# Two of four block merges moved into later links of the recurrence, and the mask add of the next sequence moved to a step's end

## The chip, the cores and the metric

The kernel runs on one core of a Trainium2 chip. The metric is the device time of one execution in microseconds. Each core has TensorE (PE: matrix products; PEld is its loading of weights), VectorE (DVE), ScalarE (ACT) and GpSimdE (POOL); each works through its own queue of instructions in order, and they wait for each other on semaphores. SyncE (SP) issues the DMAs here.

## The reference

One layer in float32, for 8 sequences of 512 tokens and width 128: a layer norm, an attention part with 8 heads of 64, a residual, and a mixture of experts. The attention is a gated delta rule in 8 modes per head. Keys and queries are turned by a mode's own angles; then, per head and mode:

```python
def step(S, inp):
    q_t, k_t, v_t, b_g, b_beta = inp
    S = S * jnp.exp(b_g)[..., None, None]
    kv = jnp.einsum('mbhk,mbhkv->mbhv', k_t, S)
    dv = (v_t[None] - kv) * b_beta[..., None]
    S = S + k_t[..., :, None] * dv[..., None, :]
    o_t = jnp.einsum('mbhk,mbhkv->mbhv', q_t, S)
    return (S, o_t)
```

The modes' outputs are summed with softmax weights.

## The kernel before

There are three stages. `prepare` (until some 810 us of the profiled execution) makes norms, projections, decay sums and angle tables. `recurrence` (until some 4640 us) runs the delta rule. `experts` does the rest. The change touches `recurrence` alone.

`recurrence` goes over 64 (head, batch) sequences of 512 tokens. The 8 modes lie as 4 pairs (`PAIRS`) on 128 partitions. A sequence is cut into 8 spans (`SUPER`) of 64 tokens. Within a span the rule is solved at once: a 64 x 64 lower-triangular system, whose inverse is built from 32 x 32 blocks. Between spans a chain of 8 links carries the state `S`.

`emit` writes a loop body of 8 steps. In step k the chain of one sequence runs while the next sequence is prepared. The bodies are: one step that only prepares (first sequence), then 7 passes of a loop (one per head) with 8 steps each, then a last body of 8. Each ends with an all-engine barrier (`fresh`).

Preparing, in order: VectorE turns keys and queries (`rotate`, L773 to L781, from `kqT`), four quarters. TensorE computes eight blocks of scores (`scores`, L929 and L933) into `SP`; ScalarE makes the decay factors of each block in place in `DB` (`exponential(c)`, L681, four instructions); VectorE multiplies both into `SC` (`take_scores`, L806), and needs for block c the scores and the exponential of c. `DB` is loaded with decay sums; GpSimdE adds `below`, the mask above the diagonal, to all of it first (L864). After the eighth block VectorE inverts the 32 x 32 diagonal blocks (`to_lanes`, then `eliminate`, L822 and L823, 30 rounds of two), and writes them back by two transposes: `TM` (L834) and `XO` (L835, `from_lanes`). The last L823 raises `lanes_done`.

Running begins with that inverse. The 64 x 64 inverse needs its lower left block, `-inverse x scores x inverse`, in two rounds m, for two halves g of the spans (g = 0 is spans 0 to 3, g = 1 is 4 to 7). `merge(0, g)` on TensorE (L910, 64 recorded products of 32 x 32) reads `TM` and the old scores in `SC` and writes `PR[g]`; ScalarE's `merged(0, g)` takes it, negated, into `ZM` (L659); `merge(1, g)` (L912, 64 recorded products) takes `ZM` and `XO`; `merged(1, g)` copies it into `XN` (L661). `first_block(e)` copies `XO` into `XN` (L665). Semaphore `act_m` counts these six on ScalarE.

A link c of the chain is, on TensorE: `solve_values` (L970), `read_state` (L958), `outputs` (L1001, L1011), `solve_reads` (L979), `keep_state` (L984), `write_state` (L994); on ScalarE: R (L726), Sdec (L730), the W copy (L733, waits for `solve_reads`), the S copy (L739, waits for `write_state`). Links 0 to 3 need half g = 0 alone, links 4 to 7 half g = 1.

The order of each queue is written out by hand. `jobs` is a list of the work that isn't chain; `PE_PLACES` and `ACT_PLACES` hold, for each link, how many jobs go to its two places. On TensorE the places of link c are ahead of `solve_reads(c)` (for c = 0 ahead of `solve_values(0)`) and behind `keep_state(c)`, ahead of `write_state(c)`. On ScalarE they are behind the W copy and behind the S copy.

Before, TensorE does merges (0,0), (0,1), (1,0) ahead of the links; then score block 0, `solve_values(0)`, merge (1,1), score block 1, `write_state(0)`; block 2, `solve_reads(1)`, `keep_state(1)`, block 3, `write_state(1)`; blocks 4 and 5, then 6 in link 2; block 7 in link 3 ahead of `solve_reads(3)`. ScalarE does `first_block(0)`, (0,0), `first_block(1)`, (0,1), exponential 0, (1,0), exponentials 1 and 2; (1,1) behind W copy 0, exponential 3 behind S copy 0, 4 and 5 in link 1, 6 and 7 in link 2 (7 behind its S copy).

Of the kernel before, what the change touches and what calls it, by code (L numbers as in the profile page):

```python
# [489 lines left out]
def recurrence(nc, sems, fresh, c_mat, ident, KQ_s, V_s, G_s, EG_s, COL_s, TAB_s, O_s):  # L490

    GROUP = SUPER // 2
    with ExitStack() as ctx:
# [61 lines left out]
        def emit(n0, h0, odd, steps, first=False):  # L555
# [17 lines left out]
            with nc.Block() as block:  # L573
# [74 lines left out]
                def _(act):  # L648
                    token_rows = PR[0][:, :].rearrange("p (z a f) -> p z a f", z=2, a=PAIRS)
                    for k, (runs, prepares, more) in enumerate(steps):  # L650
                        now, par = parts(k)

                        def merged(m, g):

                            cs = slice(GROUP * g, GROUP * g + GROUP)
                            act.wait_ge(pe_m, 4 * k + 2 * m + g + 1)
                            got = PR[g][:, :].rearrange("p (a c i) -> p a c i", a=PAIRS, c=GROUP)
                            if m == 0:
                                act.activation(ZM[:, :, cs, 0:C], got, ACT.Copy, scale=-1.0).then_inc(act_m, 1)  # L659
                            else:  # L660
                                act.copy(XN[:, :, cs, C:], got).then_inc(act_m, 1)  # L661
# [14 lines left out]
                        def exponential(c):  # L676
                            if c == 0:
                                act.wait_ge(d_ready, k + 1)
                                act.wait_ge(l_col, 16 * (k + 1))
                            for p in range(PAIRS):  # L680
                                last = act.activation(DB[:, p, c, :], DB[:, p, c, :], ACT.Exp, bias=col[:, par, 0, p, c:c + 1])  # L681
                            last.then_inc(d_exp, 1)
# [12 lines left out]
                        if runs:  # L695
# [5 lines left out]
                            merged(0, 1)  # L701
                            if prepares:
                                exponential(0)
                            merged(1, 0)
                            if prepares:
                                exponential(1)
                                exponential(2)
                        jobs = [lambda: merged(1, 1)] if runs else []
                        if prepares:
                            ex = [lambda c=c: exponential(c) for c in range(3 if runs else 0, SUPER)]  # L710
                            keys = [lambda c=c: token_keys(c) for c in range(SUPER)]
                            turn = [(lambda r=r: transposed(k + sets, r)) if more else (lambda: None) for r in range(4)]
                            jobs += ex + keys[0:4] + turn[0:2] + keys[4:6] + turn[2:3] + keys[6:8] + turn[3:4]
                        if not runs:
                            for job in jobs:
                                job()
                        else:
                            plan = ACT_PLACES if prepares else [1] + [0] * (2 * SUPER - 1)
# [136 lines left out]
                def _(pool):  # L855
                    for k, (_, prepares, _) in enumerate(steps):
                        if not prepares:
                            continue
                        if k:

                            pool.wait_ge(lanes_done, k)
                        here(pool, l_gr, 4, k)
                        every = DB[:, :, :, :].rearrange("p a c i -> p (a c) i")
                        pool.tensor_tensor(every, every, bcast(below[:, :], 1, PAIRS * SUPER), ALU.add).then_inc(d_ready, 1)  # L864

                @block.tensor
                def _(pe):
                    wins = turned = 0
                    token_rows = PR[0][:, :].rearrange("p (z a f) -> p z a f", z=2, a=PAIRS)
                    for k, (runs, prepares, more) in enumerate(steps):  # L870
# [20 lines left out]
                        def merge(m, g):  # L891

                            if m == 0 and k:
# [3 lines left out]
                                else:  # L897
                                    pe.wait_ge(act_t, 4 * turned)
                            if m == 1:
                                pe.wait_ge(act_m, 6 * k + 2 + 2 * g)  # L900
# [36 lines left out]
                        def token_keys(c2):  # L937
# [4 lines left out]
                            elif runs:  # L942
                                pe.wait_ge(act_m, 6 * k + 5)
# [17 lines left out]
                        def solve_values(c):  # L961
# [3 lines left out]
                            if c % GROUP == 0:  # L965
                                pe.wait_ge(act_m, 6 * k + 5 + c // GROUP)
# [47 lines left out]
                        if first and k == 0:  # L1014
                            wins += 1
                            for r in range(4):
                                transposes(0, r)
                        if runs:
                            merge(0, 0)
                            merge(0, 1)  # L1020
                            merge(1, 0)
                        jobs = [lambda: merge(1, 1)] if runs else []
                        if prepares:
# [5 lines left out]
                            jobs = sc[0:1] + jobs + sc[1:] + kd[0:2] + turn[0:2] + kd[2:3] + turn[2:3] + kd[3:4] + turn[3:4]  # L1029
# [3 lines left out]
                        else:  # L1033
                            plan = PE_PLACES if prepares else [0, 1] + [0] * (2 * SUPER - 2)
# [26 lines left out]
        PE_PLACES = [1, 2, 1, 1, 2, 1, 1, 1, 0, 0, 1, 1, 1, 1, 1, 1]  # L1061
        ACT_PLACES = [1, 1, 1, 1, 1, 1, 0, 0, 1, 1, 1, 2, 1, 1, 2, 0]
# [305 lines left out]
```

## Time and profile before

| | |
|---|---|
| median of 3 runs | 5335.73 us (5333.28 to 5338.02) |
| the profiled execution | 5332.65 us |
| its span, first to last instruction | 5331.1 us |
| mean granted TensorE clock | 0.835 |
| busy PE, PEld, DVE, ACT, POOL | 4090.7, 3347.1, 3758.0, 2856.6, 413.9 us |

Times in rows are us from the span's start. An entry such as `x64` counts instructions; `[1.70 <-DVE run_TM L834]` is idle time of the engine ahead of the instruction and what ended it. The granted clock is 1.00 for 2.4 GHz and 0.50 for 1.2 GHz. Ends of matrix products are modelled, so I go by starts where I can.

### The profile page before, as it was taken

The numbers are of one execution on the slowest core, as the hardware profiler recorded it, in microseconds if no ns is written. First come the engines' busy times: TensorE is split into PE (matmuls) and PEld (weight loads), VectorE is DVE, ScalarE is ACT, GpSimd is POOL, SyncE is SP. The second block draws the span as 40 slices with busy tenths as digits, with TensorE's granted clock in tenths as the row PEclk, the third lists the DMA queues.
The fourth block names the chain that finished last, engine by engine and source line by source line (L and its number), as shares of the span: only waits on it lengthen the run. The fifth ranks groups of instructions, "written<-read, shape, count | busy, mean of one in ns | idle before, by whom it ended". The sixth has DMA issues, their size and how long they took to land. (4 is left out here: it accounts for less than half of the span.)

```text
span 5331.1 us, 196493 instructions
## 1 busy us (share of the span) xinstructions
PE 4090.7 (77%) x85809; PEld 3347.1 (63%) x85809; DVE 3758.0 (70%) x7820; ACT 2856.6 (54%) x9665; POOL 413.9 (8%) x164
## 2 busy tenths in 40 slices
PE   3333006989899889989989998989899889868778
PEld 1111005777777777777777777777777777744445
DVE  3333558888888788878878887887888888534444
ACT  3333224666666666666666665666666666522222
POOL 0000321000100010000000010000100010000000
PEclk7666557888888898888889888988888889878888
DMA  2333342222222322322222222222222222120110
GB/s 62 85 85 83 143 172 60 50 63 80 50 50 60 81 51 50 88 54 50 48 81 58 52 82 47 50 63 79 50 50 63 78 50 50 24 54 14 28 28 16
DMA packets 275624, 331.13 MB, mean 62 GB/s; under 512 B 132440, under 2 KB 179424, under 8 KB 266592
## 3 DMA queue, kind: packets, MB, share of 16 engines
q1 hardware_dynamic: 274784, 318.75, 23.0%
q8 instruction: 671, 10.99, 0.9%
q14 instruction: 169, 1.38, 0.1%
HBM read 232.70 MB, written 85.98 MB: 60 GB/s over the span
## 5 line engine op out<-in xcount | busy, mean ns | idle before, releaser
L823 DVE TENSOR_TENSOR run_XL<-run_XL,run_EL 128x30 f32<-128x30 f32 (+14 forms) x1920 | 637.3, 332 | 65.9
L822 DVE TENSOR_TENSOR run_EL<-run_AL,run_XL 128x30 f32<-128x30 f32 (+14 forms) x1920 | 636.1, 331 | 66.0
L806 DVE TENSOR_TENSOR run_SC<-run_SP,run_DB 128x512 f32<-128x512 f32 x512 | 349.9, 686 | 455.7 <-PE run_SP L933 449.5
L929 PE MATMUL run_SP<-run_KP 64*32 64x128 f32 x8192 | 624.9, 302 | 23.9 <-DVE run_SC L806 10.4
L864 POOL TENSOR_TENSOR run_DB<-run_DB,run_below 128x2048 f32<-128x2048 f32 x64 | 297.2, 4644 | 3495.1 <-DVE run_XL L823 2993.9
L681 ACT ACTIVATE run_DB<-run_DB,run_col 128x64 f32<-128x64 f32 x2048 | 537.2, 337 | 13.6 <-POOL run_DB L864 5.9
L887 PE MATMUL run_PR<-ident,run_win 128*64 128x128 f32 x4096 | 303.7, 285 | 305.0 <-DMA run_win<-KQ_s 280.9
L929 PEld LDWEIGHTS run_SP<-run_KP 64*32 64x32 f32 x8192 | 467.5, 119 | 100.6 <-issue 53.1
L688 ACT ACTIVATE run_KD<-run_PR,run_col 128x64 f32<-128x64 f32 x2048 | 469.7, 326 | 12.9 <-PE run_PR L949 6.8
L739 ACT COPY run_S<-run_KS 128x256 f32<-128x256 f32 x448 | 166.7, 372 | 564.9 <-PE run_KS L994 564.9
L933 PE MATMUL run_SP<-run_KP 64*32 64x64 f32 x8192 | 454.5, 243 | 0.0
L887 PEld LDWEIGHTS run_PR<-ident,run_win 128*64 128x64 f32 x4096 | 242.1, 142 | 335.8 <-DMA run_win<-KQ_s 281.3
L726 ACT ACTIVATE run_R<-run_KS,run_col 128x64 f32<-128x64 f32 x1792 | 414.6, 322 | 70.6 <-PE run_KS L958 70.4
L773 DVE TENSOR_TENSOR run_tmpv<-run_tab,run_kqT 128x512 f32<-128x512 f32 x512 | 383.1, 748 | 76.0 <-issue 27.5
L912 PE MATMUL run_PR<-run_XO,run_ZM 32*64 32x32 f32 x8192 | 404.7, 268 | 26.6 <-ACT run_ZM L659 24.7
L730 ACT ACTIVATE run_Sdec<-run_S,run_decay 128x64 f32<-128x64 f32 x1536 | 413.4, 364 | 0.0
L912 PEld LDWEIGHTS run_PR<-run_XO,run_ZM 32*64 32x64 f32 x8192 | 387.8, 194 | 40.1 <-ACT run_ZM L659 29.6
L970 PE MATMUL run_WP<-run_V,run_XN 64*64 64x64 f32 x8192 | 374.3, 238 | 9.8 <-issue 9.0
L949 PE MATMUL run_PR<-ident,run_KP 64*64 64x64 f32 x8192 | 297.0, 222 | 95.9 <-ACT run_KD L688 90.5
L1001 PE MATMUL run_OB<-run_W,run_SC 128*64 128x64 f32 x4096 | 360.9, 234 | 0.5 <-ACT run_W L733 0.5
L949 PEld LDWEIGHTS run_PR<-ident,run_KP 64*64 64x64 f32 x8192 | 262.7, 135 | 150.4 <-issue 146.2
L979 PE MATMUL run_WP<-run_R,run_XN 64*64 64x64 f32 x7168 | 307.6, 224 | 53.6 <-ACT run_R L726 34.0
(201 smaller groups left out, 7817.7 us busy)
## 6 DMA issues: line engine op xcount, KB each, us to landing
run_DB<-G_s SPq DMA_DIRECT2D x256, 256.0 KB, 4.7
run_EG<-EG_s SPq DMA_DIRECT2D x128, 512.0 KB, 8.5
TAB_s<-tab_tab SPq DMA_DIRECT2D x16, 2048.0 KB, 6.3
run_tab<-TAB_s SPq DMA_DIRECT2D x32, 1024.0 KB, 10.8
KQ_s<-proj_win SPq DMA_DIRECT2D x32, 768.0 KB
run_win<-KQ_s SPq DMA_DIRECT2D x64, 384.0 KB
run_V<-V_s SPq DMA_DIRECT2D x128, 128.0 KB, 2.6
V_s<-proj_vv SPq DMA_DIRECT2D x64, 128.0 KB
```

Source lines behind the costliest of these rows:

```text
L681: last = act.activation(DB[:, p, c, :], DB[:, p, c, :], ACT.Exp, bias=col[:, par, 0, p, c:c + 1])
L688: last = act.activation(KD[:, par, p, c, :], token_rows[:, c % 2, p, :], ACT.Copy, scale=col[:, par, 2, p, c:c + 1])
L726: last = act.activation(R[:, p, :], KS[:, 0, p, :], ACT.Copy, scale=col[:, now, 1, p, c:c + 1])
L730: last = act.activation(Sdec[:, p, :], S[:, c % 2, p, :], ACT.Copy, scale=decay[:, now, p, c:c + 1])
L773: v(dve.tensor_tensor(tmpv[:, query], tab[:, at, :, t], bcast(kqT[:, at, t], 1, PAIRS), ALU.mult))
L822: v.link(dve.tensor_tensor(e, bcast(AL[:, r + 1:, r], 2, done), bcast(XL[:, r, 0:done], 1, rows), ALU.mult))
L823: less = dve.tensor_tensor(XL[:, r + 1:, 0:done], XL[:, r + 1:, 0:done], e, ALU.subtract)
L887: last = pe.matmul(PR[1][64 * e:64 * e + 64, 128 * i:128 * i + 128], win[:, i, off:off + DK], ident[:, :], start=True, stop=True)
L912: last = pe.matmul(to[64 * e:64 * e + SPAN], ZM[two, p, c, :], XO[two, p, c, :], start=True, stop=True)
L929: pe.matmul(out[64 * e:64 * e + C, p].rearrange("p (z u) i -> p z (u i)", z=2), KP[f, par, p, t0:t1], KP[f, kq, p, t0:t0 + SPAN], start=Tr ...
L933: last = pe.matmul(out[64 * e + C:64 * e + SPAN, p, 0::3, :], KP[f, par, p, t1:t1 + C], KP[f, kq, p, t1:t1 + C], start=True, stop=True)
L949: last = pe.matmul(token_rows[f, z, p, :], KP[f, par, p, t0:t0 + SPAN], ident[f, f], start=True, stop=True)
```

## The change

On TensorE merges (0,0) and (1,0) stay ahead of the links; (0,1) goes between `solve_values(0)` and score block 1, and (1,1) between `keep_state(1)` and score block 3. `PE_PLACES[3]` becomes 2. On ScalarE `merged(0, 1)` goes behind W copy 0, `merged(1, 1)` behind W copy 1; exponentials 0 to 2 stay ahead of the links, 3 stays behind S copy 0, 4 is behind S copy 1, 5 and 6 in link 2, and 7 behind W copy 3 (`ACT_PLACES[6]` becomes 1). The waits on `pe_m` and `act_m` are counted anew. On GpSimdE the mask add for the next sequence is issued at the end of the step before, so that the one for a pass's first step is done ahead of the barrier.

```diff
                         def merged(m, g):
...
-                            act.wait_ge(pe_m, 4 * k + 2 * m + g + 1)
+                            act.wait_ge(pe_m, 4 * k + 2 * g + m + 1)
...
                             if c == 0:
-                                act.wait_ge(d_ready, k + 1)
+                                if k + sets:
+                                    act.wait_ge(d_ready, k + sets)
                                 act.wait_ge(l_col, 16 * (k + 1))
...
                             first_block(0)
                             merged(0, 0)
                             first_block(1)
-                            merged(0, 1)
+                            merged(1, 0)
                             if prepares:
                                 exponential(0)
-                            merged(1, 0)
-                            if prepares:
                                 exponential(1)
                                 exponential(2)
-                        jobs = [lambda: merged(1, 1)] if runs else []
+                        jobs = [lambda: merged(0, 1)] if runs else []
...
+                            if runs:
+                                jobs += ex[0:1] + [lambda: merged(1, 1)]
+                                ex = ex[1:]
                             jobs += ex + keys[0:4] + turn[0:2] + keys[4:6] + turn[2:3] + keys[6:8] + turn[3:4]
+                        elif runs:
+                            jobs += [lambda: None, lambda: merged(1, 1)]
...
-                            plan = ACT_PLACES if prepares else [1] + [0] * (2 * SUPER - 1)
+                            plan = ACT_PLACES if prepares else [1, 1, 1] + [0] * (2 * SUPER - 3)
...
                 @block.gpsimd
                 def _(pool):
-                    for k, (_, prepares, _) in enumerate(steps):
-                        if not prepares:
-                            continue
-                        if k:
-
-                            pool.wait_ge(lanes_done, k)
-                        here(pool, l_gr, 4, k)
+                    def only_below(loads):
+
+                        pool.wait_ge(l_gr, 16 * 4 * loads)
                         every = DB[:, :, :, :].rearrange("p a c i -> p (a c) i")
                         pool.tensor_tensor(every, every, bcast(below[:, :], 1, PAIRS * SUPER), ALU.add).then_inc(d_ready, 1)
+
+                    if first:
+                        only_below(1)
+                    for k, (_, prepares, more) in enumerate(steps):
+                        if more:
+
+                            pool.wait_ge(lanes_done, k + 1)
+                            only_below(k + 1 + sets)
...
-                                    pe.wait_ge(act_t, 4 * turned)
+                                    pe.wait_ge(act_t, 4 * turned_so_far)
                             if m == 1:
-                                pe.wait_ge(act_m, 6 * k + 2 + 2 * g)
+                                pe.wait_ge(act_m, 6 * k + 2 + 3 * g)
...
-                                pe.wait_ge(act_m, 6 * k + 5)
+                                pe.wait_ge(act_m, 6 * k + 4)
...
-                                pe.wait_ge(act_m, 6 * k + 5 + c // GROUP)
+                                pe.wait_ge(act_m, 6 * k + 4 + 2 * (c // GROUP))
...
+                        turned_so_far = turned
                         if runs:
                             merge(0, 0)
-                            merge(0, 1)
                             merge(1, 0)
-                        jobs = [lambda: merge(1, 1)] if runs else []
+                        jobs = []
...
-                            jobs = sc[0:1] + jobs + sc[1:] + kd[0:2] + turn[0:2] + kd[2:3] + turn[2:3] + kd[3:4] + turn[3:4]
+                            if runs:
+                                jobs = sc[0:1] + [lambda: merge(0, 1)] + sc[1:3] + [lambda: merge(1, 1)] + sc[3:]
+                            else:
+                                jobs = sc
+                            jobs += kd[0:2] + turn[0:2] + kd[2:3] + turn[2:3] + kd[3:4] + turn[3:4]
+                        elif runs:
+                            jobs = [lambda: merge(0, 1), lambda: merge(1, 1)]
...
-                            plan = PE_PLACES if prepares else [0, 1] + [0] * (2 * SUPER - 2)
+                            plan = PE_PLACES if prepares else [0, 1, 0, 1] + [0] * (2 * SUPER - 4)
...
-        PE_PLACES = [1, 2, 1, 1, 2, 1, 1, 1, 0, 0, 1, 1, 1, 1, 1, 1]
-        ACT_PLACES = [1, 1, 1, 1, 1, 1, 0, 0, 1, 1, 1, 2, 1, 1, 2, 0]
+        PE_PLACES = [1, 2, 1, 2, 2, 1, 1, 1, 0, 0, 1, 1, 1, 1, 1, 1]
+        ACT_PLACES = [1, 1, 1, 1, 1, 1, 1, 0, 1, 1, 1, 2, 1, 1, 2, 0]
```

## Rows read from the trace of the kernel before

**Rows 1.** The page: busy time per engine; costliest group that waits on scores.

```profile
PE 4090.7 (77%) x85809; PEld 3347.1 (63%) x85809; DVE 3758.0 (70%) x7820; ACT 2856.6 (54%) x9665; POOL 413.9 (8%) x164
...
L806 DVE TENSOR_TENSOR run_SC<-run_SP,run_DB 128x512 f32<-128x512 f32 x512 | 349.9, 686 | 455.7 <-PE run_SP L933 449.5
```

**Rows 2.** Line L834: its instructions (ns min/median/max, first and last start), who waited (us, times).

```profile
L834 DVE STREAM_TRANSPOSE run_TM<-run_XL x64: 2012/2080/2164, 854.7 to 4615.3; 128x1024 f32<-128x1024 f32 x64
...
  PEld run_PR L910: 70.4, 39
```

**Rows 3.** Timeline (start, length in us, engine, line, ...), VectorE, two steps.

```profile
1991.97 2.06 DVE L834 STREAM_TRANSPOSE run_TM<-run_XL 128x1024 f32<-128x1024 f32 x1
...
2048.31 2.04 DVE L834 STREAM_TRANSPOSE run_TM<-run_XL 128x1024 f32<-128x1024 f32 x1
2050.27 1.93 DVE L835 STREAM_TRANSPOSE run_XO<-run_XL 128x1024 f32<-128x1024 f32 x1
...
2082.68 0.69 DVE L806 TENSOR_TENSOR run_SC<-run_SP,run_DB 128x512 f32<-128x512 f32 x1 [2.69 <-PE run_SP L933]
...
2108.26 2.10 DVE L834 STREAM_TRANSPOSE run_TM<-run_XL 128x1024 f32<-128x1024 f32 x1
```

**Rows 4.** Timeline, TensorE, the second of these steps.

```profile
2050.41 2.36 PE L910 MATMUL run_PR<-run_TM,run_SC 32*32 32x32 f32 x128 [1.70 <-DVE run_TM L834]
2053.82 3.62 PE L912 MATMUL run_PR<-run_XO,run_ZM 32*64 32x32 f32 x64 [1.04 <-ACT run_ZM L659]
...
2081.54 0.30 PE L929 MATMUL run_SP<-run_KP 64*32 64x128 f32 x2
...
2082.53 0.68 PE L979 MATMUL run_WP<-run_R,run_XN 64*64 64x64 f32 x16
```

**Rows 5.** Timeline, ScalarE, around the eighth take of that step.

```profile
2080.29 1.06 ACT L681 ACTIVATE run_DB<-run_DB,run_col 128x64 f32<-128x64 f32 x4
...
2083.26 0.37 ACT L733 COPY run_W<-run_WP 128x256 f32<-128x256 f32 x1 [0.15 <-PE run_WP L979]
2085.45 0.37 ACT L739 COPY run_S<-run_KS 128x256 f32<-128x256 f32 x1 [1.82 <-PE run_KS L994]
```

**Rows 6.** Stretches: length; busy PE, PEld, DVE, ACT, POOL; granted clock; DMA share, GB/s.

```profile
2060.00:2064.00 4.00, 4.00 (x78) 3.82 (x78) 4.00 (x8) 0.44 (x2) 0.00 (x0) 0.50 0.01 4
```

**Rows 7.** Timeline, TensorE, merges at either clock, in three other steps.

```profile
1217.14 2.05 PE L912 MATMUL run_PR<-run_XO,run_ZM 32*64 32x32 f32 x64
...
2003.80 2.35 PE L912 MATMUL run_PR<-run_XO,run_ZM 32*64 32x32 f32 x64
...
4617.38 3.62 PE L910 MATMUL run_PR<-run_TM,run_SC 32*32 32x32 f32 x128 [4.38 <-DVE run_TM L834]
```

**Rows 8.** Stretches T + 12.6 to T + 17.0, the first and last of 62.

```profile
927.80:932.20 4.40, 4.40 (x82) 3.83 (x81) 3.67 (x7) 0.58 (x1) 0.00 (x0) 0.50 0.00 0
...
4569.90:4574.30 4.40, 4.40 (x120) 4.03 (x120) 4.40 (x9) 1.74 (x6) 0.00 (x0) 0.84 0.00 0
```

**Rows 9.** Timeline, VectorE and TensorE, two steps in which the chain came late.

```profile
1688.58 2.07 DVE L834 STREAM_TRANSPOSE run_TM<-run_XL 128x1024 f32<-128x1024 f32 x1
1696.01 1.18 PE L912 MATMUL run_PR<-run_XO,run_ZM 32*64 32x32 f32 x34
...
4557.34 2.07 DVE L834 STREAM_TRANSPOSE run_TM<-run_XL 128x1024 f32<-128x1024 f32 x1
4564.52 3.62 PE L912 MATMUL run_PR<-run_XO,run_ZM 32*64 32x32 f32 x64
```

**Rows 10.** Timeline, GpSimdE within a pass; then three engines at a pass's start.

```profile
2048.36 4.57 POOL L864 TENSOR_TENSOR run_DB<-run_DB,run_below 128x2048 f32<-128x2048 f32 x1 [51.77 <-DVE run_XL L823]
...
2289.10 4.49 POOL L864 TENSOR_TENSOR run_DB<-run_DB,run_below 128x2048 f32<-128x2048 f32 x1 [60.18 <-POOLq L103]
2296.11 3.41 PE L910 MATMUL run_PR<-run_TM,run_SC 32*32 32x32 f32 x119 [2.53 <-issue]
2300.18 1.06 ACT L681 ACTIVATE run_DB<-run_DB,run_col 128x64 f32<-128x64 f32 x4
```

## The prediction

> **What bounds the kernel now.** I read the page's groups first. TensorE is the busiest engine over the span, and VectorE's largest wait is for `run_SP` at L806, the multiply that takes the scores [rows 1]. The span is then 63 repeats of one step: the first transpose of the inverses (L834, called T here) starts 64 times from 854.7 to 4615.3 us, so a step takes 59.7 us on average, and 3761 of the 5331 us go by T [rows 2]. The timeline of one step says what sets it. After T, VectorE turns keys and queries, takes eight score blocks, and from the eighth on does nothing but the elimination until the next T: the eighth was taken at 2082.68, the next T came at 2108.26, 25.6 us that have no wait in them [rows 3]. So a step is 25.6 us plus the way from T to the eighth take (34.4 us here).
>
> That way belongs to TensorE. It gets `TM` at T + 2.1 and does both merges of round 0 in the time in which ScalarE can't yet give it `ZM`; merge (1,0) starts at T + 5.5, released by ScalarE. From there the queue is full to the eighth score block, which starts at 2081.54 and is over when L979 starts at 2082.53, 0.15 us ahead of VectorE's take [rows 4]. ScalarE isn't late: its eighth exponential runs from 2080.29 to 2081.35 [rows 5].
>
> The granted clock comes in on top. In this stretch it is 0.50 (1.2 GHz) while TensorE shows no idle time at all (4.00 of 4.00 us busy) [rows 6]. It fell after the thin stretch around T, and rose only behind the second score block and link 0's writes and reads. There are two sorts of step. Between T + 12.6 and T + 17.0 the clock was 0.84 or more in 19 of 62 steps and 0.50 in the other 43 (7 of these are the first steps of a loop pass); the first and the last step are in [rows 8]. I call them short and long. The long step above lasted 59.95 us, the short one ahead of it 56.34 [rows 3].
>
> **Part 1: merge (0,1) goes behind score block 0.** Before, it ran while TensorE waited for `ZM`, at no cost. Merge (1,0) still starts at T + 5.5, since ScalarE's first block and `ZM` copy are unchanged and `ZM` released it. So merge (0,1) is now inside the full queue. Two such merges took 2.36 us at the full clock [rows 4] and 3.62 us at half [rows 7]: 1.2 or 1.8 us each. That is the cost of cover lost; nothing else fills the hole at T + 3.3.
>
> **Part 2: merge (1,1) goes behind `keep_state(1)`.** Its work is the same, but in a long step it leaves the stretch at half clock: 3.62 us become 2.05 [rows 4, 7], a gain of 1.6. A short step had it at nearly full clock already (2.35 us, [rows 7]), a gain of nothing. Together with part 1: +1.2 us in a short step, 1.8 - 1.6 = +0.2 us in a long one. In the long one the second score block and link 0's dense work also come 1.8 us sooner (3.62 out, 1.8 in), and the clock rose behind just these; if it rises sooner by that much, some 0.8 us is won. It may rise at the same time as now. I take 0.3 of this, so -0.1 us. Ends: -0.6 (that 0.8 in full) to 1.8 us per step (both merges at half clock).
>
> Here a rule of the Trainium skill speaks otherwise. The page "TensorE: Matmul & The Clock Gate" (Part 1, the HAM clock gate) ties the half clock to an idle engine and the full one to a busy engine; by this rule a merge in a full queue is as good as a score block, its place changes no clock, and both sorts of step would cost the same 1.2 us. The trace disagrees as far as it goes, with half clock and no idle time [rows 6]. By the rule this part would sum to 55 x 1.2 = 66 us instead of the 19 below, and the time to about 5500.
>
> **Part 3: ScalarE's order.** Each exponential from the fifth on moves back by one place, and `ACT_PLACES` gets a 1 behind link 3's W copy. The eighth exponential now stands behind that copy instead of behind the S copy before it. The W copy waits for L979, and L979 stands behind the eighth score block in TensorE's queue. So the exponential can't be done before the scores any more. From the rows: W copy at 2083.26, 0.37 long, four exponentials 1.06, so done at 2084.69 instead of 2081.35, against the take at 2082.68 [rows 3, 5]: VectorE waits 2.0 us more, and this sum hangs on the eighth block whenever it comes. Queued behind it on ScalarE is the next S copy, at 2085.45, so the chain isn't touched [rows 5]. It applies to all 63 steps. Bounds: 1.9 (copy and exponentials overlap a little) to 2.1.
>
> **Part 4: what the late chain takes back.** PE's weight loads waited for T's transpose in 39 of the 63 steps [rows 2]. Of the other 24, 8 are first steps of a pass, and in 16 TensorE's own chain came late: in these merge (1,0) starts at T + 7.4 (1688.58 to 1696.01) or T + 7.2 (the last one, 4557.34 to 4564.52) instead of T + 5.5 [rows 4, 9]. There VectorE's 2.0 us more let the chain catch up, by some 1.75 us each: -28 us in all (-15 to -40).
>
> **Part 5: the mask add at a step's end.** Inside a pass nothing moves: the add waited for the last L823 before and still does. It moves at the 8 starts of a pass only. There it ran at 2289.10, and the first exponential came at 2300.18, 6.6 us after its end, since instruction starts of TensorE (L910 at 2296.11) are what holds the start up [rows 10]: no gain. At the end of a pass the add runs from T + 0.05 to T + 4.6, past VectorE's second transpose, which ends at T + 3.9 [rows 3, 10], and the barrier waits for both: +0.7 us. With part 3 and 0.1 for the merges, a start of a pass costs 2.8 us (1.0 to 4.5; merge (1,0) may start up to 1 us sooner there).
>
> **The sum.** 55 steps x 2.0 = 110. Merges: 19 short x 1.2 = 23 and 36 long x -0.1 = -4, so 19. Late chain -28. Eight starts x 2.8 = 22. Together +123 us. The profiled execution took 5332.65 us (span 5331.1), 3.1 below the median of the runs, 5335.73, which I leave aside: 5455 us.
>
> **Rivals.** (a) The clock falls again. Merge (1,1) is sparse work and now stands alone amid the links, where no half clock was before. If it costs half of what parts a long from a short step (3.6 / 2 = 1.8 us) in most steps, 80 us more: 5535. For it: half clock beside merges in [rows 6]. Against: score blocks stand close on both sides of it. (b) TensorE's chain rules every step, as in the 16, and VectorE's wait is absorbed. Then merges and barriers alone count: 19 + 8 x 0.8, so about 5358. Against: 39 steps in which the chain waited for VectorE. (c) The reordering changes nothing that is seen: the exponential hides in slack and the merges cancel, 5333. Against: VectorE has no slack behind the eighth take [rows 3]. (d) Faster, by the clock. If all long steps turn short, 36 x 3.6 = 130 come off while the merge costs 1.2 in all 55: 110 + 66 - 130 - 28 + 22 = +40, still slower. It decides from 0.7 us per step beyond that: if merge (1,0) ran at the full clock too (1.6 us each, 86 us), the time would be 5287. For it: less sparse work ahead of the dense. Against: the new hole in TensorE's queue before merge (1,0) lies just where the clock falls.
>
> **Chances.** Forecast as summed 0.69; (a) 0.13, (b) 0.08, (c) 0.05, (d) 0.05. The range's low end, 5375, is the sum with the low bounds of all parts (6 off the exponentials, 18 off the merges, 12 off the chain, 14 off the starts: 5405) and ten of the long steps turned short (10 x 2.6, with the dearer merge, off that, and 4 for rounding); its high end, 5540, takes in (a). It leaves out (b), (c) and (d), 18 in 100. About 0.2% (11 us) is what a measurement of this kernel can tell from no change: faster 0.05, same 0.05, slower 0.90.
>
> **What would show it.** Right: L806's eighth take follows ScalarE's L681 instead of TensorE, 2 us after L979's start, in every step; merge (1,0) still at T + 5.5; fewer late chains. Wrong: an eighth take still released by `run_SP`; T to T below 58 us in most steps; granted clock at full by T + 10 (then d); half clock behind merge (1,1) (then a).

## The result

The changed kernel took 5509.82 us (median of 4 runs, 5507.32 to 5516.53), the kernel before 5334.5 us beside it. The ratio is 1.0338, with a 95% interval of 1.0312 to 1.0364: 175 us slower. I had said slower, 5455 us (5375 to 5540). The sign and the cost of the eighth exponential behind W copy 3 (I call that place the gate) held, and so did the time that late chains take back; 55 us of the loss were missing in the sum.

The profiled execution has a span of 5505.6 us. Lines of its page: busy times, the take of scores (L806 before, L810 now, [rows 1]), and the longest waits of VectorE from the list of waits (total us, times, longest).

```profile
PE 4118.7 (75%) x85809; PEld 3367.1 (61%) x85809; DVE 3752.3 (68%) x7820; ACT 2854.2 (52%) x9665; POOL 414.2 (8%) x164
...
L810 DVE TENSOR_TENSOR run_SC<-run_SP,run_DB 128x512 f32<-128x512 f32 x512 | 347.3, 686 | 651.5 <-ACT run_DB L682 335.0
```

```profile
DVE run_SC L810 <- ACT run_DB L682: 335.0, 191, 5.6
DVE run_SC L810 <- PE run_SP L941: 316.6, 140, 4.0
```

VectorE does the same work in 6 us less busy time, and waits 651.5 instead of 455.7 us for its takes. That is 196 us more, against the 175 of the whole. Of the 651.5 us, 335.0 are waits for exponentials, which came to 5.8 us before.

The new T is the start of L838. The line's own view, as in [rows 2]:

```profile
L838 DVE STREAM_TRANSPOSE run_TM<-run_XL x64: 2008/2058/2170, 854.9 to 4787.4; 128x1024 f32<-128x1024 f32 x64
...
  PEld run_PR L918: 143.8, 50
```

T to T is now 62.4 us on average ((4787.4 - 854.9) / 63) instead of 59.7: 171.9 of the 175 us lie between the first T and the last. Of this the 8 starts of a pass have 18 us and the 55 other steps 153.

One step, as in [rows 3 to 5]: timelines of VectorE, TensorE and ScalarE.

```profile
2043.63 2.03 DVE L838 STREAM_TRANSPOSE run_TM<-run_XL 128x1024 f32<-128x1024 f32 x1
...
2079.45 0.69 DVE L810 TENSOR_TENSOR run_SC<-run_SP,run_DB 128x512 f32<-128x512 f32 x1 [2.55 <-ACT run_DB L682]
...
2105.04 2.05 DVE L838 STREAM_TRANSPOSE run_TM<-run_XL 128x1024 f32<-128x1024 f32 x1
...
2166.53 2.06 DVE L838 STREAM_TRANSPOSE run_TM<-run_XL 128x1024 f32<-128x1024 f32 x1
```

```profile
2045.72 1.20 PE L918 MATMUL run_PR<-run_TM,run_SC 32*32 32x32 f32 x64 [3.48 <-DVE run_TM L838]
2049.07 3.62 PE L920 MATMUL run_PR<-run_XO,run_ZM 32*64 32x32 f32 x64 [2.16 <-ACT run_ZM L659]
...
2055.52 1.92 PE L918 MATMUL run_PR<-run_TM,run_SC 32*32 32x32 f32 x64
...
2064.45 2.05 PE L920 MATMUL run_PR<-run_XO,run_ZM 32*64 32x32 f32 x64
...
2077.29 0.68 PE L987 MATMUL run_WP<-run_R,run_XN 64*64 64x64 f32 x16
```

```profile
2078.02 0.37 ACT L737 COPY run_W<-run_WP 128x256 f32<-128x256 f32 x1 [0.15 <-PE run_WP L987]
2078.29 1.06 ACT L682 ACTIVATE run_DB<-run_DB,run_col 128x64 f32<-128x64 f32 x4
```

The order of events at the end of the way is plain: L987 starts at 2077.29, the W copy at 2078.02, the exponentials end at 2079.35, the take comes at 2079.45. It is 2.16 us behind L987, in this step and in all others; before it was 0.15 us behind L979 [rows 3, 4]. All 63 eighth takes are released by L682; before, all 63 were by `run_SP`. Merge (1,0) starts at T + 5.4, as forecast; merge (0,1) takes 1.92 at half clock, merge (1,1) 2.05 at full.

What I hadn't seen coming is in the spacing. T to T is 61.41 and 61.49 in these two steps, and between 61.0 and 61.8 in all 55 that aren't a pass's first. Before, [rows 3] had 56.34 and 59.95 in a row. The stretches T + 12.6 to T + 17.0 and T + 17.5 to T + 21.9 of two steps (columns as in [rows 6]):

```profile
2056.20:2060.60 4.40, 4.40 (x106) 3.83 (x102) 4.40 (x8) 1.20 (x4) 0.00 (x0) 0.50 0.02 4
2061.10:2065.50 4.40, 4.40 (x120) 3.67 (x118) 4.03 (x8) 2.88 (x13) 0.00 (x0) 1.00 0.30 89
2117.60:2122.00 4.40, 4.40 (x106) 3.82 (x102) 4.40 (x8) 1.20 (x4) 0.00 (x0) 0.50 0.01 4
2122.50:2126.90 4.40, 4.40 (x120) 3.67 (x117) 4.03 (x8) 2.96 (x13) 0.00 (x0) 0.99 0.31 93
```

The clock comes back at T + 17.5 in step after step (from T + 17.4 to T + 17.9 in all 55). I will say that a step rises early when the clock is back at full by T + 14. Before, 18 of 55 did, and lasted 56.5 us on average; the other 37, which I call late, lasted 59.7. (These are the prediction's short and long steps, but for one that rose 0.03 us behind the mark.) In the changed kernel none is early.

### The profile page after: what moved, and what is told of

It is laid out like the page before. It is cut to its first block and busy times, and to the rows that moved or that the text cites. A ratio compares the mean times of both kernels' runs of the same rounds, so it can differ in the third digit from the quotient of the medians.

```text
span 5505.6 us, 196493 instructions
## 1 busy us (share of the span) xinstructions
PE 4118.7 (75%) x85809; PEld 3367.1 (61%) x85809; DVE 3752.3 (68%) x7820; ACT 2854.2 (52%) x9665; POOL 414.2 (8%) x164
## 5 line engine op out<-in xcount | busy, mean ns | idle before, releaser
L810 DVE TENSOR_TENSOR run_SC<-run_SP,run_DB 128x512 f32<-128x512 f32 x512 | 347.3, 686 | 651.5 <-ACT run_DB L682 335.0
L937 PE MATMUL run_SP<-run_KP 64*32 64x128 f32 x8192 | 643.4, 309 | 17.4 <-DVE run_SC L810 9.9
L682 ACT ACTIVATE run_DB<-run_DB,run_col 128x64 f32<-128x64 f32 x2048 | 530.3, 336 | 12.8 <-POOL run_DB L864 5.1
L941 PE MATMUL run_SP<-run_KP 64*32 64x64 f32 x8192 | 466.0, 247 | 0.0
L920 PE MATMUL run_PR<-run_XO,run_ZM 32*64 32x32 f32 x8192 | 357.4, 252 | 107.9 <-ACT run_ZM L659 107.9
L920 PEld LDWEIGHTS run_PR<-run_XO,run_ZM 32*64 32x64 f32 x8192 | 341.8, 174 | 136.7 <-ACT run_ZM L659 115.4
L978 PE MATMUL run_WP<-run_V,run_XN 64*64 64x64 f32 x8192 | 387.4, 243 | 20.6 <-issue 19.8
L918 PE MATMUL run_PR<-run_TM,run_SC 32*32 32x32 f32 x8192 | 211.8, 219 | 228.3 <-DVE run_TM L838 125.0
L978 PEld LDWEIGHTS run_WP<-run_V,run_XN 64*64 64x64 f32 x8192 | 337.2, 157 | 45.9 <-issue 45.9
```

The lines of the kernel that those rows point to most:

```text
L920: last = pe.matmul(to[64 * e:64 * e + SPAN], ZM[two, p, c, :], XO[two, p, c, :], start=True, stop=True)
L937: pe.matmul(out[64 * e:64 * e + C, p].rearrange("p (z u) i -> p z (u i)", z=2), KP[f, par, p, t0:t1], KP[f, kq, p, t0:t0 + SPAN], start=Tr ...
L941: last = pe.matmul(out[64 * e + C:64 * e + SPAN, p, 0::3, :], KP[f, par, p, t1:t1 + C], KP[f, kq, p, t1:t1 + C], start=True, stop=True)
L978: last = pe.matmul(WP[f, 0, p, :], XN[f, p, c, :], V[f, now, c, :], start=(p == 0), stop=(c == 0 and p == PAIRS - 1))
```

## The experiments

My theory: each eighth exponential costs 2 us, the merges little, and where the clock comes back decides what a step costs. The rivals: the merges' place is the loss; the gate hides; the mask add matters. All numbers "against before" are ratios to the kernel before run on the same chip, with the 95% interval; where a loss or gain in us follows such a ratio, it is worked out from it. The experiments ran on several chips, on which the kernel before took 5334 to 5347 us, so differences between experiments are only good to some 10 us. Numbers of steps are of one profiled execution each.

### The gate taken out of the changed kernel

```diff
                                 exponential(1)
                                 exponential(2)
+                                exponential(3)
...
-        ACT_PLACES = [1, 1, 1, 1, 1, 1, 1, 0, 1, 1, 1, 2, 1, 1, 2, 0]
+        ACT_PLACES = [1, 1, 1, 1, 1, 1, 0, 0, 1, 1, 1, 2, 1, 1, 2, 0]
```

> The changed kernel, with exponential 3 put in the head of ScalarE's queue so that all later ones move up by one place and the eighth stands behind S copy 2 again, as before the change. Merges and mask add stay as changed. Theory (the eighth exponential behind W copy 3 costs VectorE 2 us a step): the eighth take follows TensorE again, each step loses 2.0 us, 63 x 2.0 = 126 us less than the changed kernel's 5509.8: about 5384. Some 28 us of it may be given back as late chains: 5384 to 5412. Rival (the merges' place and the clock are the whole loss, the exponential would be late anyway): the time stays within 20 us of 5510. If the clock's rise at T + 17.5 in every step was tied to the step's length, short steps come back and it gets below 5370.

5321.31 us, against before 0.9969 (0.9953 to 0.9984). So taking the exponential's place back removes the whole loss and more, and the rest of the change is a small gain of some 17 us. All 63 eighth takes are released by TensorE again; this is one of them:

```profile
2130.50 0.69 DVE L811 TENSOR_TENSOR run_SC<-run_SP,run_DB 128x512 f32<-128x512 f32 x1 [2.68 <-PE run_SP L942]
```

It gave back 188 us (197 by the two ratios) and not 126. The last sentence of the expectation is what happened: 37 of 55 steps rise early. These last 57.6 us, the other 18 last 59.65. Against before that is +1.1 and -0.1: my prices for the moved merges in a short and in a long step (+1.2, -0.1) were right to a tenth. Their gain is that more steps rise early. TensorE's longer hole ahead of merge (1,0) is in this kernel too, so that hole isn't what keeps the changed kernel's steps late.

### The gate alone

```diff
-        ACT_PLACES = [1, 1, 1, 1, 1, 1, 0, 0, 1, 1, 1, 2, 1, 1, 2, 0]
+        ACT_PLACES = [1, 1, 1, 1, 1, 0, 1, 0, 1, 1, 1, 2, 1, 1, 2, 0]
```

> The kernel before, with the eighth exponential alone moved behind W copy 3 (ACT_PLACES 1,1,1,1,1,0,1,0 in the first eight places). Nothing else. Theory: 2.0 us a step in 63 steps, less some 28 us that late chains take back: about 5432 (5415 to 5460). Rival (it only costs together with the moved merges): within 15 us of 5334. A rival on the clock (a longer step alone makes all steps long ones, without any moved merge): 19 short steps turn long, 40 to 70 us more, 5470 to 5505.

5457.88 us, against before 1.0231 (1.0178 to 1.0284): 123 us. That lies between the 98 of my sum and the clock rival's 136 and more, and the interval, 95 to 152 us, takes in both. The steps decide: they grew by 1.8 us, early ones from 56.5 to 58.3 and late ones from 59.7 to 61.5, and 15 instead of 18 rise early, so most of the early steps stayed. A part of this kernel does what the changed one does throughout. Three T in a row:

```profile
2881.24 2.13 DVE L834 STREAM_TRANSPOSE run_TM<-run_XL 128x1024 f32<-128x1024 f32 x1
...
2942.74 2.04 DVE L834 STREAM_TRANSPOSE run_TM<-run_XL 128x1024 f32<-128x1024 f32 x1
...
3004.26 2.07 DVE L834 STREAM_TRANSPOSE run_TM<-run_XL 128x1024 f32<-128x1024 f32 x1
```

61.50 and 61.52 us, with the clock's rise at T + 20.0 each time. For three passes in a row (21 steps behind their first ones) no step was early, without any moved merge.

### Merge (1,1) alone

```diff
+                            if runs:
+                                jobs = ex[0:2] + jobs
+                                ex = ex[2:]
...
-                            jobs = sc[0:1] + jobs + sc[1:] + kd[0:2] + turn[0:2] + kd[2:3] + turn[2:3] + kd[3:4] + turn[3:4]
+                            if runs:
+                                jobs = sc[0:3] + jobs + sc[3:]
...
-        PE_PLACES = [1, 2, 1, 1, 2, 1, 1, 1, 0, 0, 1, 1, 1, 1, 1, 1]
+        PE_PLACES = [1, 1, 1, 2, 2, 1, 1, 1, 0, 0, 1, 1, 1, 1, 1, 1]
```

> The kernel before, with merge (1,1) alone moved behind keep_state(1) (exponentials 3 and 4 ahead of its copy, the eighth still behind S copy 2); merge (0,1) stays ahead of (1,0), and the mask add where it was. Theory (half clock is what the early place costs): a long step gains 1.6 to 2.4 us, a short one nothing, 36 x 2 = 72 us less than before: about 5262 (5235 to 5290). Rival (the merge, sparse, pulls the clock down wherever it stands): no gain, 5320 to 5400, with half clock behind it in the links.

5252.15 us, against before 0.9845 (0.9816 to 0.9873): 83 us less. Merge (1,0), the first row, is still at half clock, but merge (1,1), the second, runs at full:

```profile
2027.90 3.62 PE L915 MATMUL run_PR<-run_XO,run_ZM 32*64 32x32 f32 x64 [1.18 <-ACT run_ZM L659]
...
2041.27 2.05 PE L915 MATMUL run_PR<-run_XO,run_ZM 32*64 32x32 f32 x64
```

Late steps fell from 59.7 to 58.1, early ones stayed (56.6), and 30 instead of 18 are early. The clock doesn't fall behind the merge; my rival (a) is wrong.

### The mask add alone

```diff
-                                act.wait_ge(d_ready, k + 1)
+                                if k + sets:
+                                    act.wait_ge(d_ready, k + sets)
...
-                        if k:
...
-                            pool.wait_ge(lanes_done, k)
-                        here(pool, l_gr, 4, k)
...
+                        if more:
...
+                            pool.wait_ge(lanes_done, k + 1)
+                            only_below(k + 1 + sets)
```

> The kernel before, with the mask add alone moved to the end of the step before (GpSimdE's block and ScalarE's wait as in the change). Theory (it only reaches the barrier at the end of a pass, 0.7 us later than VectorE): +0 to +8 us, 5334 to 5343. Rival (the add was in the way of a pass's first steps, VectorE's first product there took 2.27 us beside it): 10 to 20 us less, 5315 to 5325.

5338.57 us, against before 1.0003 (0.9982 to 1.0025). No effect that can be told from none; the 6 us of the sum wouldn't be seen. The profiled execution does show the first steps of a pass 0.7 us longer (67.3 against 66.7 on average), as forecast. It also has 23 early steps instead of 18 at the same time, so a few early steps more or less say nothing by themselves.

### Merge (0,1) alone

From the kernel with the gate taken out (so exponential 3 stays in the head of ScalarE's queue, and the mask add stays as changed):

```diff
-                                jobs += ex[0:1] + [lambda: merged(1, 1)]
-                                ex = ex[1:]
+                                jobs += [lambda: merged(1, 1)]
...
-                                jobs = sc[0:1] + [lambda: merge(0, 1)] + sc[1:3] + [lambda: merge(1, 1)] + sc[3:]
+                                jobs = sc[0:1] + [lambda: merge(0, 1)] + sc[1:2] + [lambda: merge(1, 1)] + sc[2:]
...
-        PE_PLACES = [1, 2, 1, 2, 2, 1, 1, 1, 0, 0, 1, 1, 1, 1, 1, 1]
+        PE_PLACES = [1, 3, 1, 1, 2, 1, 1, 1, 0, 0, 1, 1, 1, 1, 1, 1]
...
-        ACT_PLACES = [1, 1, 1, 1, 1, 1, 0, 0, 1, 1, 1, 2, 1, 1, 2, 0]
+        ACT_PLACES = [2, 1, 1, 1, 1, 0, 0, 0, 1, 1, 1, 2, 1, 1, 2, 0]
```

> Merge (0,1) moved behind solve_values(0) as in the change, but merge (1,1) still ahead of write_state(0) (order: score block 0, solve_values(0), merge (0,1), score block 1, merge (1,1), write_state(0)); the eighth exponential stands ahead of W copy 3, so it is no gate; mask add as changed. It is the move of merge (0,1) alone. Theory (the hole ahead of merge (1,0) stays empty and the merge costs 1.2 us in a short and 1.8 in a long step): 19 x 1.2 + 36 x 1.8 = 88 us, less 15 for late chains: 5334 + 73 = about 5407 (5380 to 5440). Rival (the hole is filled by something else, or the merge hides behind a wait of TensorE in link 0): within 15 us of 5334.

5391.65 us, against before 1.0101 (1.0060 to 1.0142): 54 us more. Early steps cost 57.9 (+1.4) and late ones 62.1 (+2.3), dearer than I said, but 35 steps are early; with 18 early steps, as before, it would have been some 110 us (18 x 1.4 + 37 x 2.3). The lost cover is in the rows: TensorE's hole ahead of merge (1,0) grew from 1.04 [rows 4] to 1.97 us.

```profile
2077.65 3.63 PE L920 MATMUL run_PR<-run_XO,run_ZM 32*64 32x32 f32 x64 [1.97 <-ACT run_ZM L659]
2084.10 1.92 PE L918 MATMUL run_PR<-run_TM,run_SC 32*32 32x32 f32 x64
2087.80 3.62 PE L920 MATMUL run_PR<-run_XO,run_ZM 32*64 32x32 f32 x64
```

The four parts alone come to 123 - 83 + 54 + 0 = 94 us, with intervals of 11 to 28 us on each, some 40 together. Together they cost 175 (180 by the ratio). The missing 80 are in no part.

### More work on VectorE in the changed kernel

```diff
                             dve.wait_ge(scored, SUPER * (k + 1))
+                            for _ in range(2):
+                                v.link(dve.tensor_tensor(tmpv[:, 0], tmpv[:, 0], tmpv[:, 1], ALU.max))
```

> The changed kernel, with two more VectorE instructions of 0.68 us (a maximum of 512 columns into the spare half of tmpv, its value unused) behind the eighth take in every step: 1.3 us more in the part of the step that only VectorE sets. Theory (each step of the changed kernel ends with the clock rising at the same point, T + 17.5, because a step of 61.44 us keeps its place to the clock's changes; another length breaks that and short steps come back): less than half of the added time shows, at most 40 us over 5510, and several steps with a rise before T + 13. Rival (the moved merges make every step a long one by themselves, whatever its length): all of it shows, 64 x 1.3 = 83 us, about 5593, and the rise stays behind T + 16 in nearly all steps.

5512.12 us, against before 1.0323 (1.0305 to 1.0342). That is 2 us over the changed kernel by the medians and a little under it by the ratio: no difference. The added work stands in the part of a step that nothing hides, and is run in every step. It takes 1.42 us there, 91 us in 64 steps:

```profile
1517.60 0.69 DVE L810 TENSOR_TENSOR run_SC<-run_SP,run_DB 128x512 f32<-128x512 f32 x1 [2.54 <-ACT run_DB L682]
1518.32 1.42 DVE L817 TENSOR_TENSOR run_tmpv<-run_tmpv 128x512 f32<-128x512 f32 x2
1519.78 1.93 DVE L818 STREAM_TRANSPOSE run_AL<-run_SC 128x1024 f32<-128x1024 f32 x1
```

And it costs nothing that shows in the whole, since the steps are unequal again. Four T in a row, and the stretch T + 12.6 to T + 17.0 of the same steps:

```profile
1483.58 2.04 DVE L840 STREAM_TRANSPOSE run_TM<-run_XL 128x1024 f32<-128x1024 f32 x1
...
1544.63 2.04 DVE L840 STREAM_TRANSPOSE run_TM<-run_XL 128x1024 f32<-128x1024 f32 x1
...
1607.37 2.07 DVE L840 STREAM_TRANSPOSE run_TM<-run_XL 128x1024 f32<-128x1024 f32 x1
...
1668.12 2.05 DVE L840 STREAM_TRANSPOSE run_TM<-run_XL 128x1024 f32<-128x1024 f32 x1
```

```profile
1496.20:1500.60 4.40, 4.39 (x156) 3.88 (x154) 4.40 (x8) 2.84 (x11) 0.00 (x0) 0.98 0.01 4
1557.20:1561.60 4.40, 4.40 (x110) 3.82 (x108) 4.40 (x8) 1.21 (x4) 0.00 (x0) 0.54 0.00 0
1620.00:1624.40 4.40, 4.39 (x158) 3.88 (x151) 4.40 (x8) 3.19 (x13) 0.00 (x0) 1.00 0.02 4
1680.70:1685.10 4.40, 4.39 (x160) 3.88 (x160) 4.40 (x8) 2.93 (x11) 0.00 (x0) 1.00 0.01 4
```

61.05, 62.74 and 60.75 us: the early steps are shorter than those of the changed kernel although they hold 1.4 us more. 37 of 55 are early. The eighth take comes at T + 34.5 on average, 1.4 sooner than in the changed kernel. So "every step late" is no property of the moved merges: with the same merges and a step 1.42 us longer, early steps come back. It goes with a step of some 61.44 us, as in the three passes of the kernel with the gate alone.

### Dense products in TensorE's holes

```diff
+                        def busy(n):
+                            for _ in range(n):
+                                pe.matmul(WP[:, 1].rearrange("p a v -> p (a v)")[:, 0:128], ident[:, :], ident[:, :], start=True, stop=True)
...
                         if runs:
+                            if k:
+                                busy(8)
                             merge(0, 0)
                             merge(0, 1)
+                            busy(4)
                             merge(1, 0)
```

> The kernel before, with dense products whose result is never read (identity times identity, 128 x 128, into the unused half of WP) in TensorE's two holes around T: 8 ahead of merge (0,0) (all steps but a pass's first) and 4 between merges (0,1) and (1,0). All waits and orders else are as before. Theory (the step's front is at half clock because TensorE was thinly used around T): the clock stays at full or rises early, all steps become short or shorter: at least 36 x 3.6 = 130 us less, about 5200 (5100 to 5230). Rival (the clock's fall can't be held off by 2 us of products, and they only take queue time): 0 to 60 us more than 5334.

5203.63 us, against before 0.9753 (0.9730 to 0.9776): 136 us less, for work whose result nobody reads. In 36 of 55 steps the clock was never at half between T and the eighth take. Merge (1,0) took 2.05 instead of 3.62 us there. The theory had all steps early; 42 of the 55 were. L893 are the added products:

```profile
2472.78 2.05 PE L893 MATMUL run_WP<-ident 128*128 128x128 f32 x16
2474.76 2.21 PE L914 MATMUL run_PR<-run_TM,run_SC 32*32 32x32 f32 x128
2476.90 1.16 PE L893 MATMUL run_WP<-ident 128*128 128x128 f32 x8
2478.07 2.05 PE L916 MATMUL run_PR<-run_XO,run_ZM 32*64 32x32 f32 x64
```

```profile
2482.00:2486.00 4.00, 4.00 (x133) 3.69 (x130) 4.00 (x8) 2.03 (x7) 0.00 (x0) 1.00 0.01 4
```

### The same in the kernel with merge (1,1) moved

The diff is those of "Merge (1,1) alone" and of the dense products above, together.

> The same dense products (8 and 4) in the kernel with merge (1,1) alone moved (5252 us). Theory: if the products keep the clock up, merge (1,1) has no half clock to leave, and this comes out like the dense kernel before, within 30 us of it; if they don't, it stays at 5252 to 5310. Rival (both gains add up in full): 130 us below 5252, about 5120.

5163.4 us, against before 0.9669 (0.9651 to 0.9686). It is 40 us under the dense kernel before: between what the theory allowed (30) and the rival (83). The clock was never at half in 45 of 55 steps now instead of 36. So moving the merge still helps the clock stay up, though it has little half clock to leave.

### Sparse products as a control

```diff
+                            for i in range(n):
+                                one = slice(64 * (i % 2), 64 * (i % 2) + C)
+                                pe.matmul(WP[64 * (i % 2) + C:64 * (i % 2) + SPAN, 1, 0, 0:C], ident[one, one], ident[one, 0:C], start=True, stop=True)
...
+                                busy(56)
...
+                            busy(28)
```

> Control to the dense products in the kernel before: in the same two places (ahead of merge (0,0), between merges (0,1) and (1,0)) 56 and 28 products of 32 x 32 in place of 8 and 4 of 128 x 128, about the same 2 and 1 us of TensorE time, result never read. Theory (what keeps the clock up is dense work; filled time alone doesn't): the clock falls in every step as before and the products cost some queue time, 5334 to 5400. Rival (any work in the holes keeps the clock up): 130 us less than before, as with the dense ones, about 5205.

5518.2 us, against before 1.0329 (1.0286 to 1.0371), above what either side expected. In this form work in the holes doesn't do it: the clock fell in every step, and only 3 were early. But as a control it is flawed. The 84 small products stand in TensorE's queue as 168 recorded ones, and behind them it stood idle in the middle of a merge, which the profile puts down to "issue": to nothing that it shows. TensorE had 59 such gaps ahead of this line, 122 us in all, against 19 and 68 us in the dense kernel, where 60 of the 68 us fall in the first steps of passes:

```profile
2096.90 0.53 PE L915 MATMUL run_PR<-run_TM,run_SC 32*32 32x32 f32 x11 [1.95 <-issue]
```

Merge (1,0) starts at T + 8.7 on average. What part of the clock's fall is the sparse work and what part this gap, the run doesn't tell.

### Dense products in the changed kernel

```diff
                         if runs:
+                            if k:
+                                busy(8)
                             merge(0, 0)
+                            busy(8)
                             merge(1, 0)
```

> The changed kernel with dense products in TensorE's holes (8 ahead of merge (0,0) in all steps but a pass's first, 8 between merges (0,0) and (1,0)). It shows what the change costs where the clock isn't in it. Theory: the dense kernel before (5204) plus 2.0 us for the exponential and 1.2 us for merge (0,1) in some 55 steps, less what late chains take back (34 of 55 steps were late there): 5204 + 176 - 60 = about 5320 (5280 to 5380). Rival (the longer hole lets the clock fall in spite of the products): above 5430.

5300.17 us, against before 0.9926 (0.9899 to 0.9954). That is 97 us over the dense kernel before (92 by the ratios) instead of 175. But the two aren't alike: this one has 8 and 8 dense products, that one 8 and 4, and the clock was at half for 1.4 us of a step's way to the eighth take here and 2.9 there. Early steps alone last 57.9 us here and 55.0 there, 2.8 us more. So the 97 us aren't the change's price at full clock; some of that price is made up for by late steps that are gone (none here, 13 there). All 63 eighth takes are still released by the exponential.

### No products in a pass's first step

```diff
-                            busy(4)
+                            if k:
+                                busy(4)
```

> The fastest kernel so far (merge (1,1) alone moved, dense products 8 and 4; 5163) without the 4 products in a pass's first step, where TensorE is behind by itself and the clock is at half. There merge (1,0) began 2.3 us later than without them: 8 x 1.7 to 8 x 2.3 us less, about 5147 (5140 to 5155). Rival (the first step is late by its instructions' arrival, not by the products): 5163.

5170.64 us, against before 0.9679 (0.9653 to 0.9706), beside 0.9669 of the kernel it started from: no gain. The first steps did get 2.3 us shorter (67.6 to 65.3 on average), and the other 55 lost 0.4 each: merge (1,0) started at T + 7.15 on average instead of T + 6.71, and the clock was at half at some point in 16 of them instead of 10. I don't know what makes them so.

### Dense products and no gate in the changed kernel

The diffs of "The gate taken out of the changed kernel" and of "Dense products in the changed kernel".

> The changed kernel with dense products in TensorE's holes (8 and 8, as in the run of 5300 us) and, besides, exponential 3 in the head of ScalarE's queue, so that the eighth stands behind S copy 2 again. The clock is near full in both, so the difference is the price of the exponential's place without the clock. Theory: 2.0 us a step, less what late chains take back (0.6 us a step or more, since TensorE's chain is the next bound): 63 x 1.2 to 63 x 2.0 = 76 to 126 us less than 5300, 5174 to 5224. The 188 us that undoing it gave in the changed kernel would then have been 2.0 us a step and some 60 us of clock. Rival (the place costs 188 us by itself, through ScalarE or the chain): about 5112.

5251.81 us, against before 0.9847 (0.9831 to 0.9863): 48 us under the gated one (42 by the ratios), less than either side expected. The undoing has a price of its own at full clock. Four exponentials now stand ahead of W copy 0, and `write_state(0)` (L1007) has to wait for it. In the lists of waits, weight loads and products, of this kernel and then of the gated one:

```profile
PEld run_KS L1007 <- ACT run_W L738: 57.2, 49, 1.4
PE run_KS L1007 <- ACT run_W L738: 44.2, 43, 1.2
```

```profile
PEld run_KS L1006 <- ACT run_W L737: 16.1, 34, 0.5
PE run_KS L1006 <- ACT run_W L737: 6.9, 33, 0.2
```

Some 37 to 41 us of such waits are new. With them added, the gate would be worth 85 to 89 us with the clock out of it, which is within the theory's 76 to 126. That addition is argued, not run.

## Why the prediction was right, and where it fell short

**Part 3, the gate.** Right in mechanism and nearly in size: 2.16 - 0.15 = 2.01 us between the two distances to L987 and L979. Alone it costs 123 us (95 to 152), where the sum had 110 + 16, less the 28 of part 4.

**Part 4, late chains.** Right. In the 55 steps merge (1,0) starts at T + 5.58 on average, before at T + 6.08: 55 x 0.5 = 28 us, as summed. PE's weight loads now wait for T's transpose in 50 steps instead of 39.

**Part 5, the mask add and a pass's start.** 18 us where 22 were summed; the add alone makes no difference in the time.

**Parts 1 and 2, the merges.** The prices per step were right: 1.92 us for merge (0,1) at half clock, 2.05 for merge (1,1) at full, +1.1 in an early and -0.1 in a late step of the kernel without the gate. The step that failed is the count in "19 short x 1.2 = 23 and 36 long x -0.1". I took the numbers of short and long steps over from the kernel before. They aren't the change's to keep. With merges moved and no gate 37 are early, and the pair is a gain; with the gate on top none is. Of the 16 late chains 13 were in late steps, 3 in early ones. So the sum had the 37 late steps at 59.7 + 2.0 - 0.1 and 0.6 less for late chains, 61.0 us; they are at 61.5, which is 18 of the missing 55 us. The 18 early ones were to become 56.5 + 2.0 + 1.2 - 0.3 = 59.4 and are 61.5 as well: 18 x 2.1 = 37, the rest.

**What was luck.** The measured time lies within my range, but nearer to rival (a)'s 5535 (25 us) than to my sum (55 us). I had drawn the upper end to take in (a), and (a)'s mechanism is out. Nothing in the range stood for early steps that turn late.

**Why none is early.** In the kernel before, unequal steps shift against the clock's changes, and some fall well. A step of 61.44 us doesn't shift: the rise stands at T + 17.5 every time. And the state restores itself. Behind a pass's first step the rise stood at T + 17.7 and the step lasted 61.6 us, and one or two steps later both were back at 17.5 and 61.45: a step that is a little longer has the rise sooner in the next one, which is then shorter. In the delayed kernel 91 us more work on VectorE were made up for by early steps that came back. Three runs say that it is the step's length: with 2.0 us less (the gate taken out) and with 1.42 us more (the delay) early steps come back, and with unmoved merges and the same length (the gate alone) they are gone for three passes. How the chip times its changes isn't shown, and I leave it at what the rows show.

The Trainium skill's page "TensorE: Matmul & The Clock Gate" (Part 1, the HAM clock gate) ties half clock to an idle engine. Rows of the changed kernel disagree as those of before did: 4.40 of 4.40 us busy at 0.50. The 66 us that this rule gave for the merges would have brought my sum nearer to the result, for a wrong reason: without the gate the merges' moves are a gain of 17 us.

**The rivals.** (a) is out: no half clock behind merge (1,1); from the rise to the eighth take the clock stayed at full in all 55 steps. (b) and (c) are out by the releasers of the eighth take. (d) has half a truth: moved merges do make more steps early, but the gate undoes it.

A version that beats both kernels is the one with merge (1,1) alone moved and dense products in the holes: 5163.4 us, 3.3% under the kernel before. Without the products, 5252.15 us.

## What to carry to other kernels

Before a job moves back in a queue, ask which wait it then stands behind: here an exponential that nobody waited for was put behind a copy that waits for a product of TensorE, and that product stands in the queue behind the very scores the exponential is multiplied with. And where a loop's steps are of two sorts by TensorE's clock, the shares aren't constants: here a change of a step's length turned all of them to the worse sort, so a part's price measured alone need not add up. Work in TensorE's holes that is thrown away can be worth more than the order of the work that counts: 136 us here, against 83 for the best order tried.

## What was not expected of the hardware

This loop settled on one spacing with the clock's changes: 61.0 to 61.8 us in 55 of 55 steps, the rise at T + 17.4 to T + 17.9, where the kernel before had steps of 56 to 63 us. Out of that state, 1.42 us more of unhidden work per step cost 2 us in the whole execution. And 12 products of 128 x 128 per step, 3 us of TensorE time, kept the clock up in 36 of 55 steps, and took 136 us off.
